# Head size 8 attention: values products of both halves of a group side by side on TensorE in every other step

## The reference

```
q = (x @ wq).reshape(b, n, heads, dh).transpose(0, 2, 1, 3)
k = (ctx @ wk).reshape(b, j, heads, dh).transpose(0, 2, 1, 3)
v = (ctx @ wv).reshape(b, j, heads, dh).transpose(0, 2, 1, 3)
sim = jnp.einsum('bhid,bhjd->bhij', q, k) * scale
a = jax.nn.softmax(sim, axis=-1)
out = jnp.einsum('bhij,bhjd->bhid', a, v)
out = out.transpose(0, 2, 1, 3).reshape(b, n, heads * dh)
return out @ wo + bo
```

## Time and profile before

| what | value |
|---|---|
| runs of the kernel before | 3719.72 us (median), 3706.51, 3859.67 |
| profiled execution, its time | 3714.61 us |
| span of that execution | 3712.8 us |
| mean granted clock of TensorE | 0.989 |
| TensorE busy | 3613.0 us (97%) |
| VectorE busy | 2301.5 us (62%) |
| ScalarE busy | 2091.5 us (56%) |
| GpSimd busy | 1260.7 us (34%) |

### The profile page before, as it was taken

How to read it: one execution, slowest core, us unless ns; L and a number is a source line. 1 busy time by engine, 2 the same in 40 slices (tenths; PEclk the granted TensorE clock), 3 DMA queues, 4 the chain that set the end, 5 groups by cost and what they waited for, 6 DMA issues and landing times. The chain is left out here.

```text
span 3712.8 us, 98282 instructions
## 1 busy us (share of the span) xinstructions
PE 3613.0 (97%) x38023; PEld 3125.9 (84%) x38023; DVE 2301.5 (62%) x3916; ACT 2091.5 (56%) x5165; POOL 1260.7 (34%) x1279
## 2 busy tenths in 40 slices
PE   5999999999999999999999999899999999999999
PEld 4777777877887889889899888788888888888888
DVE  2788866665454666666666666556555555556554
ACT  2677777775344655555555555455555555555333
POOL 4333333332442333333333333333233322333442
PEclk8899999999999999999999999999999999999999
DMA  4343433321101000000000000100000000000000
GB/s 112 91 100 86 105 80 85 91 76 50 43 0 35 2 1 0 0 0 0 0 0 0 0 0 1 25 3 2 2 2 1 2 2 2 1 2 1 19 19 25
DMA packets 99546, 98.72 MB, mean 27 GB/s; under 512 B 31248, under 2 KB 74128, under 8 KB 99344
## 3 DMA queue, kind: packets, MB, share of 16 engines
q1 hardware_dynamic: 94224, 94.50, 9.8%
q0 software_dynamic: 5120, 1.35, 0.2%
HBM read 20.76 MB, written 5.24 MB: 7 GB/s over the span
## 5 line engine op out<-in xcount | busy, mean ns | idle before, releaser
L1181 POOL TENSOR_TENSOR a_probs<-a_probs,a_rsums 128x1024 f32<-128x1024 f32 x160 | 303.5, 1897 | 752.8 <-DVE a_rsums L1306 752.8
L1219 ACT ACTIVATE a_probs<-a_scores_banks,a_negmax 128x128 f32<-128x128 f32 x1280 | 366.7, 376 | 284.6 <-DVE a_negmax L1294 284.5
L1181 POOL TENSOR_TENSOR c_probs<-c_probs,c_rsums 128x616 f32<-128x616 f32 x160 | 204.2, 1276 | 758.2 <-DVE c_rsums L1306 758.2
L704 ACT ACTIVATE s_probs<-s_scoresT_banks 128x1024 f32<-128x1024 f32 (+1 forms) x320 | 327.2, 1022 | 194.3 <-PE s_scoresT_banks L877 192.1
L1219 ACT ACTIVATE c_probs<-c_scores_banks,c_negmax 128x77 f32<-128x77 f32 x1280 | 312.2, 334 | 197.4 <-DVE c_negmax L1294 197.3
L789 DVE TENSOR_REDUCE s_negmax<-s_scores_banks 128x8 f32<-128x1024 f32 (+1 forms) x320 | 322.4, 1007 | 150.2 <-PE s_scores_banks L859 146.2
L1287 DVE COPY c_outT<-c_out_bank 128x512 f32<-128x512 f32 x160 | 110.7, 692 | 367.1 <-PE c_out_bank L1466 307.0
L1287 DVE COPY a_outT<-a_out_bank 128x512 f32<-128x512 f32 x160 | 110.7, 692 | 293.1 <-PE a_out_bank L1466 239.9
L1635 DVE SCALAR_TENSOR_TENSOR f_hidden<-f_value_bank,bias,f_gate 128x512 f32<-128x512 f32 x160 | 120.1, 751 | 244.9 <-ACT f_gate L1610 243.0
L667 POOL DMA_DIRECT2D s_q_stack<-s_shift x160 | 93.5, 585 | 504.7 <-ACT s_shift L727 498.6
L1294 DVE TENSOR_REDUCE a_negmax<-a_scores_banks 128x4 f32<-128x512 f32 x320 | 206.2, 686 | 88.2 <-PE a_scores_banks L1365 88.2
(11 more groups left out here) (308 smaller groups left out, 10613.9 us busy)
## 6 DMA issues: line engine op xcount, KB each, us to landing
s_q_stack<-front SPq DMA_DIRECT2D x192, 160.0 KB, 3.3
s_k_stack<-front SPq DMA_DIRECT2D x96, 160.0 KB, 3.7
s_out<-s_heads SPq DMA_DIRECT2D x128, 80.0 KB, 2.5
s_k_stack<-front SPq DMA_DIRECT2D x96, 96.2 KB, 2.8
x_tokens<-in_x SPq DMA_DIRECT2D x16, 320.0 KB, 4.7
out_x<-x_tokens SPq DMA_DIRECT2D x16, 320.0 KB, 2.4
s_q_stack<-s_shift POOLq DMA_DIRECT2D x160, 8.0 KB, 2.7
s_ctx_in<-in_ctx SPq DMA_DIRECT2D x16, 115.5 KB
```

Source lines behind the costliest of these rows:

```text
L704: nc.scalar.activation(probs[i][0:NK, :, :], scoresT[0:NK, :, :], ACT.Exp).then_inc(s_exp, 1)
L1181: nc.gpsimd.tensor_tensor(probs[i][:], probs[i][:], rsums[(k - 1) % 2][:].unsqueeze(2).broadcast_to([P, UNIT, NK]), ALU.mult).then_inc(s_p ...
L1219: done = nc.scalar.activation(probs[i][:, h, :], scores[:, h // GROUP, h % GROUP * NK:(h % GROUP + 1) * NK], ACT.Exp, bias=negmax[k % 2][: ...
```

## The change

Before, each step of TensorE did the values products of one half-group, that of step k - 6. Now even steps do none, and odd steps do two half-groups one behind the other: the one that the even step before used to do (`k - PV_LAG - 1`, half 0), then the one of this step (half 1). No matmul is added or dropped, and no other engine's code is touched; `s_pv` is counted up by the same matmuls in the same order.

```diff
                 scores_step(k)
                 scoresT_step(k - ST_LAG)
-                values_step(k - PV_LAG)
+                if k % 2:
+                    values_step(k - PV_LAG - 1)
+                    values_step(k - PV_LAG)
                 made = maxima_at(k)
```

## The result

| | before | changed |
|---|---|---|
| median of 4 runs each, us | 3734.89 (3706.51 to 3859.67) | 3893.82 (3880.54 to 3913.88) |
| profiled execution, us | 3714.61 | 3913.88 |
| mean granted clock of TensorE | 0.989 | 0.937 |
| last scores of the small layers start at, us | 894.1 | 1090.4 |

The ratio is 1.0469, with a 95% interval of 1.0414 to 1.0524: slower by over 2%, and far outside the range given.

A forecast was written before the change was run, and what follows sets the result against it. TensorE was taken as the bound on average, with even self steps held by the wait for the maxima. Fifteen self quads at +1.2 and fifteen cross quads at +0.8 add 30 us to 3714.6: 3745, range 3693 to 3780.

The forecast's parts named there:

- The loop of scores and maxima: Self layer: with one scores buffer, scores wait for VectorE's maxima, so no even step can be shorter than 1.99 us.
- The second block: Odd steps: a second values block directly behind the first adds 0.44 us, if no gap opens.
- The 0.20 from scores to the transpose: Even steps: without values, the transpose of the maxima follows the transposed scores after a gap taken as 0.20 us.
- Step 5 "near 3.0": Self layer: odd step 5, with both values halves, would take near 3.0 us, from 2.57.
- The self quad "near 26.2": Self layer: a quad of ten steps would take near 26.2 us, net +1.2.
- The wait for `s_out` in step 4: Self layer: the earlier transpose of the maxima waits 0.2 us for VectorE's product, inside the wait for the maxima.
- TensorE's queue alone: Rival: only TensorE's queue decides, a pair of steps gains 0.13 us, 3695 us in all; chance 0.15.
- a gap between the halves: Rival: a gap of 0.2 us separates the two values halves in odd steps, 30 us more, 3775; chance 0.10.
- The cross quad: Cross layer: a quad of ten steps grows by net +0.8 us, to near 26.0.
- The five even steps: Cross layer: each even step saves 0.28 us, as estimated for step 4, together 1.40 a quad.
- The five odd steps: Each odd step grows by 0.44 us for its second values block, together 2.20 a quad.
- The granted clock falls: Rival: thinner TensorE work lowers its clock; one layer 38 us more, chance 0.08, both 75 us more, chance 0.07.

The follow-up runs named there:

- e8: Changed kernel, but steps 0 and 1 of the cross layer each do their own half as before: 3737.50 us, ratio 1.0059.
- e1: Changed kernel with the halves side by side only in the self layer, the cross layer as before: 3729.14 us, ratio 1.0048.
- e2: Changed kernel with the halves side by side only in the cross layer, the self layer as before: 3837.10 us, ratio 1.0223.
- e3: Changed kernel with 14 more filler matmuls in a cross quad, all in even steps: 3822.19 us, ratio 1.0297.
- e4: Kernel before, TensorE made to wait for the exponential after the values products in steps 4 and 6 of the cross layer: 3743.70 us, ratio 1.0108.
- e10: Kernel before, values in place, TensorE made to wait behind them for the exponential in step 0 of the cross layer: 3837.04 us, ratio 1.0324.
- e5: Changed kernel with 6 more filler matmuls in step 9 of each cross quad (10 instead of 4): 3749.85 us, ratio 1.0097.
- e12: Kernel before with 20 filler matmuls a cross quad in place of 27, ten of them in step 9: 3722.88 us, ratio 0.9991.

## Why the prediction was wrong

**What held.** The loop of scores and maxima as the floor of an even step in the self layer: 1.99 forecast, 1.98 measured. The second block: 0.44 and no gap. The 0.20 from scores to the transpose. Step 5 "near 3.0": 3.01. The self quad "near 26.2": 26.16. The wait for `s_out` in step 4: 0.25, where 0.2 was forecast. The rivals "TensorE's queue alone" and "a gap between the halves" are out by the same rows: the quads grew, and by no gap.

**What was mis-sized beside it.** The cross quad: +0.8 forecast, +1.15 measured. The five even steps give back 1.49 us, where 1.40 was forecast, but that is luck: single steps give 0.02 to 0.57 where 0.28 was taken for each. The five odd steps cost 2.64, where 2.20 was forecast; steps 7 and 9 have the excess. In step 7 the transposed scores start 0.31 us after the first scores (547.23, 547.54), where it was 0.03 before: they wait for the exponential of step 6, which ends at 547.49. The forecast had this wait, but inside the even step. By the quads the mechanism costs 15 x 1.18 + 15 x 1.15 = 35 us. By the runs it is 22 without the pair in steps 0 and 1 of the cross layer (e8), and 26.41 - 25.87 = 0.54 a quad, 8 us in fifteen, for that pair: 30, with the width of e8's interval. The forecast's 30 fits both within that width, no closer. The self layer's 18 has the same limit (6 to 30, e1).

**What failed** is that the sum took the granted clock at 1.00 throughout, and the price of the rival "The granted clock falls". I took that price from the earlier trace rows, a stretch with a mean clock of 0.90, as 10% of a layer, 38 us for one and 75 for both. That 0.90 is a mean of two levels: in those 100 us the trace of before has 20.5 us at 0.50 and the rest at 1.00. What counts is for how long the clock stays low, and the row said nothing on that. A cross quad takes 44.19 us at 0.50 and 26.41 at 1.00, so each costs 17.8 us, and nine in a row cost 160 us, twice the price of both layers. With the 30 to 35 us of mechanism that is nearly all of the 199.

How long a loss lasts varied. Ten losses in the kept traces start in a step 0 of the cross layer, 1.1 to 1.7 us into it. Nine ended in a step 1, six of them in quads 18, 23 or 28, where `BURST_QUADS` puts 12 more fillers into that step; the tenth (e2) passed the burst of quad 28 at 0.50 and ended in step 3 of the last quad, 13 us before its last scores. The changed kernel didn't get the clock back at the burst of quad 23, only at that of quad 28. In e3 it came back in quad 27, which has no burst. Seven traces, that of the kernel before among them, have one more loss, which starts in the last step 9 of the self layer; it lasts 10.2 us before and 20.5 in the changed kernel.

**The chance** was too low for a reason that was in the text. "Against it: the clock stays at 1.00 in stretches that have such waits already" was drawn from the self layer, and e4 shows the clock held in steps 4 and 6 of the cross layer too. But step 0 of the cross layer is another place, and the prediction passed it over in half a sentence ("step 0 has the wait for `s_ctx_low` ahead of its projection") and gave it the same 0.28 us as the others; it gave back 0.02. The values block there lay between two waits and covered the second. Taking it out opens 0.33 us of waiting after a stretch that has only scores. Following what a removed block had covered, at each place where it stood, would have found it. And clock 1.00 in a trace says that the clock was held, not by how much. The other side was there to see and not used: the opening's rows at 0.50 and 0.90, the 10.2 us at 0.50 at the entry into the cross layer, and a run of 3859.67 us of the kernel before.

**What stays open.** That waiting in step 0 of the cross layer brings the fall is shown (e10, and e8 for the way back). Why there is not told by these runs: TensorE is busy for 2.74 and 2.76 us of the 3.4 ahead of a fall, but for 2.77 around e4's wait in step 4, which held. The fall also depends on when step 0 comes: e10 held the clock in two quads with the same wait, and the four runs of the changed kernel differ by 33 us. In e5 the wait for the low part in step 0 stood alone, without the one for the values copy in step 9, and the profiled execution kept the clock from 512 us on; whether the filled wait or the six fillers themselves did it wasn't separated.

## What to carry to other kernels

Moving work between steps of a pipeline costs time where the steps it leaves are held by a loop (here scores and maxima, 1.98 us) and the steps it enters are held by the queue: count each step by itself, not the average. Where filler matmuls hold the clock, look at each stretch that a change thins out, not at the quad's sum alone, and price a loss by how long it lasts until the clock comes back. How thin is too thin these runs don't tell, so such a change has to be tried. Here six fillers just ahead of the sparse spot held the clock, and the same six two steps earlier, or fourteen elsewhere and behind its wait, did not.

## What was not expected of the hardware

- One wait of 0.63 us in step 0 of a quad of 26 us was enough for TensorE's clock to halve for 372 us (e10), while two such waits in other steps, which made the quad 1.5 us longer, did not halve it in 390 us (e4).
- Busy throughout, TensorE stayed at 0.50 for 283 us, 2679 matmul records, with twelve extra fillers among them (e2); in e3 the clock came back after 150 us without such a burst.
- The loss hits the same kernel in some runs and not in others: 3688.60 to 3842.24 us for e12, at mean granted clocks of 0.993 and 0.949.
